# Moving two kinds of DMA issue between queues, filling products in bf16, and new orders, in a four-layer diffusion transformer kernel

## What is computed

```python
def attention(x, kv_src, w, gate):          # seven of them in all
    h = layer_norm(x) * scale + shift       # modulated in most
    q, k, v = h @ Wq + bq, kv_src @ Wk + bk, kv_src @ Wv + bv
    s = einsum("qhd,khd->hqk", q, k) / sqrt(8)
    # five attentions are over all 256 keys, one is in shifted windows of 64 tokens,
    # one keeps the 16 largest scores of each query (top_k) before the softmax
    return x + gate * (softmax(s) @ v @ Wo + bo)

def mlp(x):                                 # three of them; gelu, gelu, swiglu
    return x + gate * (act(norm(x) @ W1 + b1) @ W2 + b2)

# blocks: self + cross + mlp; self + cross + mlp; cross; window + top-16 cross + mlp
```

## Time and profile before

| | us |
|---|---|
| median of 3 runs | 686.51 (684.52 to 690.16) |
| the profiled execution | 680.88 |
| its span, first to last instruction | 679.0 |
| mean granted TensorE clock | 0.904 of full speed |

### The profile page before, as it was taken

How to read it: one execution, slowest core, us unless ns; L and a number is a source line. 1 busy time by engine, 2 the same in 40 slices (tenths; PEclk the granted TensorE clock), 3 DMA queues, 4 the chain that set the end, 5 groups by cost and what they waited for, 6 DMA issues and landing times.

```text
span 679.0 us, 14686 instructions
## 1 busy us (share of the span) xinstructions
PE 586.4 (86%) x5250; PEld 403.1 (59%) x5250; DVE 494.0 (73%) x1291; ACT 389.6 (57%) x671; POOL 242.9 (36%) x471
## 2 busy tenths in 40 slices
PE   4879999999989998999999997999668699787587
PEld 4645565566655655667656665667335478555456
DVE  3777766754668687636876547999998997799963
ACT  3557768788797868885878775345112150421133
POOL 7951422254532232345323353145111423112133
PEclk9869979999999998999999997579665799987899
DMA  9570342203241352013222234025000000000000
GB/s 322 134 188 2 96 110 65 64 2 65 64 86 42 68 123 65 1 34 95 64 64 65 65 78 113 4 57 125 7 2 0 2 9 2 2 8 1 2 1 16
DMA packets 22230, 39.25 MB, mean 58 GB/s; under 512 B 2640, under 2 KB 6800, under 8 KB 21904
## 3 DMA queue, kind: packets, MB, share of 16 engines
q1 hardware_dynamic: 20736, 37.37, 22.6%
q10 hardware_dynamic: 1424, 0.95, 0.5%
HBM read 7.96 MB, written 0.52 MB: 12 GB/s over the span
## 4 chain that ended last, share of the span: by engine, by line
PE 44%; ACT 18%; DVE 16%; DMA 8%; issue 7%; POOL 5%; ACTq 1%; SPq 1%; POOLq 0%
PE psum L1590 9%; ACT softmax_T L1290 9%; PE psum L1472 8%; PE psum L1566 6%; DMA qk_stack<-centred 6%; DVE left L1418 4%; PE psum L1536 4%; DVE top L1415 3%; DVE left L1428 3%; DVE top L1425 3%; PE psum L1636 3%; PE psum L1625 2%; PE psum L1577 2%; ACT qk_parts L1270 2%; PE psum L1505 2%
## 5 line engine op out<-in xcount | busy, mean ns | idle before, releaser
L1290 ACT ACTIVATE softmax_T<-psum 128x1024 f32<-128x1024 f32 (+1 forms) x224 | 210.8, 971 | 119.6 <-PE psum L1577 77.2
L1405 DVE TENSOR_REDUCE maxima<-psum 128x4 f32<-128x1024 f32 x160 | 189.6, 1217 | 65.1 <-PE psum L1536 64.7
L1566 PE MATMUL psum<-qk_stack 32*128 32x256 f32 (+1 forms) x896 | 113.9, 341 | 29.2 <-ACT softmax_T L1290 9.7
L1590 PE MATMUL psum<-softmax_T,values 128*32 128x256 f32 (+1 forms) x1792 | 124.7, 395 | 5.6 <-ACT softmax_T L1290 4.0
L1566 PEld LDWEIGHTS psum<-qk_stack 32*128 32x128 f32 x896 | 72.5, 201 | 76.6 <-issue 39.2
L1219 POOL TENSOR_SCALAR unpicked<-left 128x512 bf16<-128x512 f32 x64 | 39.5, 617 | 156.2 <-DVE left L1428 155.7
L1536 PE MATMUL psum<-qk_stack 32*128 32x256 f32 (+1 forms) x768 | 86.5, 331 | 8.6 <-ACT softmax_T L1290 2.8
L1179 POOL TENSOR_TENSOR qk_parts<-qk_parts 128x256 fp32r<-128x256 f32 x56 | 40.6, 727 | 113.7 <-ACT qk_parts L1273 113.5
L1590 PEld LDWEIGHTS psum<-softmax_T,values 128*32 128x32 f32 x1792 | 56.1, 116 | 39.2 <-ACT softmax_T L1290 10.4
L1472 PE MATMUL psum<-identity 128*128 128x256 f32 x248 | 68.7, 430 | 11.0 <-DVE left L1418 10.6
L1536 PEld LDWEIGHTS psum<-qk_stack 32*128 32x128 f32 x768 | 56.2, 195 | 35.9 <-issue 16.1
(11 more groups left out here) (98 smaller groups left out, 832.1 us busy)
## 6 DMA issues: line engine op xcount, KB each, us to landing
qk_stack<-qk_parts SPq DMA_DIRECT2D x112, 256.0 KB, 4.6
weights<-in_w SPq DMA_DIRECT2D x1, 1408.0 KB, 13.3
row_biases<-in_rows SPq DMA_DIRECT2D x1, 1088.0 KB, 10.4
weights<-in_w SPq DMA_DIRECT2D x2, 512.0 KB, 5.8
weights<-in_w SPq DMA_DIRECT2D x1, 832.0 KB, 8.9
qk_stack<-centred ACTq DMA_DIRECT2D x48, 8.0 KB
weights<-in_w SPq DMA_DIRECT2D x1, 768.0 KB, 6.6
weights<-in_w SPq DMA_DIRECT2D x1, 576.0 KB, 6.6
```

The lines of the kernel that those rows point to most:

```text
L1290: nc.scalar.activation(pT[:, slot, u % 2, :, 0:cols].rearrange("p (i t) n -> p i t n", t=NT), two_banks(step).rearrange("p i (t n) -> p i ...
L1405: nc.vector.tensor_reduce(rows[:, u // 4, u // 2 % 2, g:g + 2, :], ps.rearrange("p i (t k) -> p i t k", t=NT), AX_X, ALU.max).then_inc(fin, 1)
L1566: ins = nc.tensor.matmul(ps[:, i, t, 0:P if window else N], QKS[b][32 * g:32 * g + 32, s, 1, P * t:P * t + P], QKS[b][32 * g:32 * g + 32, ...
L1590: ins = nc.tensor.matmul(misc[32 * g:32 * g + 32, queries], V[:, b, t, first:first + 32], pT[:, slot, g // 2, 2 * (g % 2) + t, 0:P if wind ...
```

## The change

- **Stacks.** The 112 DMAs of the q and k stacks are tasks of POOL in place of SP: POOL issues each behind its own two subtractions.
- **Maxima.** The 64 DMAs of the maxima are tasks of SP in place of ACT. ACT keeps the copy to SBUF; SP waits for it. ACT issues no DMA in the loop any more.
- **Filling products** read the same identity as bf16 (128 rows, 256 columns). The planner's entry for one goes from 0.24 to 0.12 us, and their number from 0.95 of a gap to the smaller of 0.85 of it and 0.3 us + 0.6 of it.
- **Orders.** The planner's entries follow (a stack 1.0 us of POOL where it was 0.57 us of SP; the maxima 0.26 us of ACT and 0.57 us of SP where they were 0.95 us of ACT), and `LEAD`, `BIAS` and `EXTRA` have new values throughout, so all five orders are new.

```diff
@@ the planner's table of durations
-    ... ("sp", "load"): 0.6, ("sp", "stack"): 0.57,
+    ... ("sp", "load"): 0.6, ("pool", "stack"): 1.0,
-    ("pe", "maxima"): 0.33, ("act", "maxima"): 0.95,
+    ("pe", "maxima"): 0.33, ("act", "maxima"): 0.26, ("sp", "maxima"): 0.57,
...
-IDLE, SPARE_SHARE, SPARE_D, SPARE_CELLS = 0.3, 0.95, 0.24, 0.2133
+IDLE, SPARE_D, SPARE_CELLS = 0.3, 0.12, 0.107
...
 EXTRA = {
...
 }
@@ plan: tasks
-            stack = [task("sp", ("stack", b, l, s), t) for s in range(4)]
+            stack = [task("pool", ("stack", b, l, s), t) for s in range(4)]
...
-                        maxed[u // 4] = task("act", ("maxima", b, l, u // 4),
-                                             task("pe", ("maxima", b, l, u // 4), t), maxed.get(u // 4 - 1))
+                        t = task("act", ("maxima", b, l, u // 4), task("pe", ("maxima", b, l, u // 4), t),
+                                 maxed.get(u // 4 - 1))
+                        maxed[u // 4] = task("sp", ("maxima", b, l, u // 4), t)
...
@@ plan: how many filling products
-                spare[step] = int((s - since) * SPARE_SHARE * (1.0 if clock.rate == 1 else 1 / 1.8) / SPARE_D)
+                spare[step] = int(min(0.85 * (s - since), 0.3 + 0.6 * (s - since)) * (1.0 if clock.rate == 1 else 1 / 1.8) / SPARE_D)
...
-        if eng == "sp" and kind == "stack":
+        if eng == "pool" and kind == "stack":
             moves = max(end + TO_QUEUE, queue)
-            free[eng] = end = max(end, moves - AHEAD)
             queue = moves + STACK_TIME
...
@@ the table LEAD (samples down, layers of the chain across)
-LEAD = [[22.6, 23.7, 18.9, 23.7, 23.1, 31.1, 24.3, 23.5, 66.9, -397.7],
-        [15.8, 16.7, 15.8, 15.7, 15.6, 15.7, 16.4, 17.6, -44.9, 1073.6],
-        [7.8, 8.2, -12.2, 7.7, 7.8, 13.7, 8.3, 5.1, -29.6, -483.8],
-        [-0.3, 0.7, 0.9, -0.2, -0.4, 13.1, 0.5, 608.1, 549.0, 112.7]]
+LEAD = [[29.6, 27.3, 159.8, 27.1, 27.2, 25.2, 30.7, 27.0, 78.1, 420.1],
+        [18.3, 18.3, 18.3, 19.7, 18.7, -13.4, -10.7, -63.6, 338.4, -332.4],
+        [9.3, 9.1, 50.8, 7.5, 8.8, 525.5, 13.5, -500.4, -1.8, 224.2],
+        [1.3, 1.4, 437.2, -0.3, 0.9, -1.2, 4.4, 87.9, 52.7, -9.6]]
@@ SP's queue
-            sp.wait_ge(q_zero_s, 1)
-            sp.wait_ge(k_rows_s, 16 * SLOTS["qk"])
             for step in ORDERS["sp"]:
                 kind, b, l, u = step
-                if kind == "stack":
-                    slot = SLOT["qk", ("k_parts", b, l, 0)][0]
-                    after(sp, "pool", ("qk", b, l, 0))
-                    after(sp, "pool", ("k_parts", b, l, 0))
-                    sp.dma_start(QKS[b][:, u, :, :].bitcast(F32),
-                                 parts[32 * u:32 * u + 32, slot, :, :, :].bitcast(F32)).then_inc(stacked[b][u], 16)
+                if kind == "maxima":
+                    after(sp, "act", step)
+                    if ATTN[l]["kind"] == "topk":
+                        sp.dma_start(QKS[b][31::32, u, 0, :].bitcast(F32),
+                                     z[0:4, b, :, :].rearrange("p t f -> p (t f)")).then_inc(max_in[b], 16)
+                    else:
+                        sp.dma_start(QKS[b][31::32, 2 * u:2 * u + 2, 0, :].bitcast(F32),
+                                     z[0:NH // 2, b, :, :].rearrange("p t f -> p (t f)")).then_inc(max_in[b], 16)
@@ POOL's queue
+            pool.wait_ge(q_zero_s, 1)
+            pool.wait_ge(k_rows_s, 16 * SLOTS["qk"])
             for step in ORDERS["pool"]:
                 kind, b, l, u = step
-                if kind == "z":
+                if kind == "stack":
+                    slot = SLOT["qk", ("k_parts", b, l, 0)][0]
+                    pool.wait_ge(done["qk", "pool"], NTH["pool", ("qk", b, l, 0)])
+                    pool.wait_ge(done["k_parts", "pool"], NTH["pool", ("k_parts", b, l, 0)])
+                    pool.dma_start(QKS[b][:, u, :, :].bitcast(F32),
+                                   parts[32 * u:32 * u + 32, slot, :, :, :].bitcast(F32)).then_inc(stacked[b][u], 16)
+                elif kind == "z":
@@ ACT's queue, kind "maxima", behind the copy
-                    act.wait_ge(fin, NTH["act", step])
-                    if ATTN[l]["kind"] == "topk":
-                        act.dma_start(QKS[b][31::32, u, 0, :].bitcast(F32),
-                                      z[0:4, b, :, :].rearrange("p t f -> p (t f)")).then_inc(max_in[b], 16)
-                    else:
-                        act.dma_start(QKS[b][31::32, 2 * u:2 * u + 2, 0, :].bitcast(F32),
-                                      z[0:NH // 2, b, :, :].rearrange("p t f -> p (t f)")).then_inc(max_in[b], 16)
@@ PE's queue
                 for _ in range(SPARE.get(step, 0)):
-                    nc.tensor.matmul(psum[:, SLOT["bank", step][0], 0:2 * P], ident[:],
-                                     ident[:].rearrange("p (o c) -> p o c", o=1).broadcast_to([P, 2, P]),
-                                     start=True, stop=True)
+                    nc.tensor.matmul(psum[:, SLOT["bank", step][0], 0:2 * P], ident[:].bitcast(BF16)[:, 0:P],
+                                     ident[:].bitcast(BF16), start=True, stop=True)
```

More of the change, by code:

```diff
@@ L189 @@
 EXTRA = {
[L190 to L199, removed]
@@ L563 @@
-    ("dve", "mods"): 46.3, ("dve", "pbias"): -3.2, ("dve", "residual"): 82.1, ("dve", "scores"): -13.4,
-    ("dve", "stats"): 10.7, ("dve", "topk"): 247.8, ("dve", "topk_rest"): 79.7, ("dve", "up_gate"): -233.8,
[3 rows of a table removed]
-    ("pool", "gated"): -7.1, ("pool", "k_parts"): 47.3, ("pool", "pre"): -6.2, ("pool", "qk"): -1.5,
-    ("pool", "topk"): 62.7, ("pool", "z"): -11.4, ("sp", "load"): -261.8, ("sp", "stack"): 24.4,
-    ("sp", "store"): 6.0,
+    ("act", "context"): -21.7, ("act", "heads_out"): 106.1, ("act", "k_parts"): 0.8, ("act", "maxima"): 50.3,
@@ L571 @@
+    ("pe", "gates"): -1.7, ("pe", "mods"): -24.4, ("pe", "normed"): 0.1, ("pe", "pbias"): 4.5, ("pe", "qk"): -0.1,
+    ("pe", "residual"): 0.1, ("pe", "topk"): 38.5, ("pe", "up"): -0.3, ("pe", "up_gate"): 184.2,
+    ("pe", "values"): 0.1, ("pool", "gated"): 0.6, ("pool", "k_parts"): -3.6, ("pool", "pre"): -11.2,
+    ("pool", "qk"): 137.4, ("pool", "stack"): -3.6, ("pool", "topk"): 283.6, ("pool", "z"): -2.3,
+    ("sp", "load"): -114.6, ("sp", "maxima"): 115.5, ("sp", "store"): 42.9,
 }
@@ L714, in plan @@
                         i = u // half
[L715 to L717 removed]
+                        t2 = task("act", ("maxima", b, l, i), task("pe", ("maxima", b, l, i), t), maxed.get(0))
+                        maxed[2 * i] = maxed[2 * i + 1] = task("sp", ("maxima", b, l, i), t2)
+            prev = mixed = copied = None
             for u in range(8):
@@ L760, in plan @@
     for t in reversed(_sorted(order, deps)):
-        tail[t] = busy(t) + (transfer(t[1]) if t[1][0] == "load" else lands.get(t[1][0], 0.0) if t[0] == "sp" else 0.0) + max(
+        tail[t] = busy(t) + (transfer(t[1]) if t[1][0] == "load" else lands.get(t[1][0], 0.0) if t[0] == "sp" or t[1][0] == "stack" else 0.0) + max(
             (tail[n] + HOP for n in users[t]), default=0.0)
@@ L803, in gives @@
             yield "bank", (kind, b, l, u // 2 * 2 if kind == "mix" else u)
-        if eng == "sp" and kind == "stack" and u == 3:
+        if eng == "pool" and kind == "stack" and u == 3:
             yield "qk", ("k_parts", b, l, 0)
@@ L905, in plan @@
             land = queue + LANDS
-        elif eng == "act" and kind == "maxima":
+        elif eng == "sp" and kind == "maxima":
             land = end + TO_QUEUE + 0.3
         for r, taker in gives(t):
-            slots[r] += [((end if kind == "maxima" else land) + HOP, k, taker) for k in slot[r, taker]]
+            slots[r] += [(land + HOP, k, taker) for k in slot[r, taker]]
             slots[r].sort()
```

403 lines of the change are left out of this document (207 added, 196 removed), and 341 rows, old and new, of tables (BIAS, EXTRA).

## The result

| | before | after |
|---|---|---|
| median of 4 runs side by side | 688.34 us (684.52 to 690.41) | 668.25 us (665.29 to 671.45) |
| ratio | | 0.9739, 95% interval 0.9688 to 0.979 |
| the profiled execution | 680.88 us | 665.29 us |
| its span | 679.0 us | 663.5 us |
| mean granted TensorE clock | 0.904 | 0.863 |

The change is faster by 2.6%, 17.9 us of 686.5, where 669 us had been forecast. A ratio is taken over each kernel's fast executions alone (within 1.5% of its fastest), so it is not the quotient of the medians; of the kernel with both moves undone, further down, three of six are left out of it.

A forecast was written before the change was run, and what follows sets the result against it. POOL sets the pace to 45 us, PE to 418, DVE to 643, then a thin tail. 680.9 - 10 - 8 - 6 + 4 + 2.5 = 663.4 us profiled, 669 us as median; range 655 to 680 (52%).

The forecast's parts named there:

- Fillings, -10 us: DVE's waits for PE's top-16 products and the tail: fillings no longer overstay gaps, -10 us, bounds -4 and -17.
- Stacks on POOL, +4 and +2.5 us: POOL's queue: four issues at 1.0 us delay the start, +4; later latency and holds, with SP's hop, +2.5.
- Maxima off ACT, -8 + 1.1 us: Before 418 us: ACT freed of issuing maxima, -8 us, bounds 0 and -28.8; SP's later issue, +1.1.
- a second stretch that ends some 10 us earlier: Sign for ACT's relief: the stretch from 45 to 418 us, where PE sets the pace, ends some 10 us earlier.
- The bound of -28.8: Most that taking maxima off ACT could gain: all of PE's idle time from 45 to 418 us, 28.8 us.
- Orders, -6 us: Edge at 418 us: one sample's window layer moves under the top-16 phase, -6 us, bounds +5 and -19.
- Overlap of the phases by three samples: Rival 1, edge at 418 us: three samples' worth of order, fillings at their bound, 649 us; 14%.
- PE as the limit: Rival 2, before 418 us: PE at 92% takes over, ACT's relief worth 3 us, 684 us; 18%.
- Rival 2: PE takes over before 418 us: ACT's relief 3 us, orders nothing, fillings 6, 684 us, within 1%; 18%.
- rivals 3 and 4: POOL's queue: POOL becomes the limit, 709 us, 11%; DVE holds up POOL's issues, some 700 us, 5%.
- POOL as the limit: Rival 3, POOL's queue, first before 45 us: issues at 1.742 us, 709 us, deciding from about 1.5; 11%.
- DVE holding up POOL's issues: Rival 4, POOL's queue: each issue waits out half a DVE reduction, costing 1.6 us, some 700 us; 5%.

## Why the prediction was right, point by point

**Fillings, -10 us: right.** 6.5 us in the old orders and 10.8 in the new. The part in DVE's wait was larger than I took (11.8 of 13.8 us, I took 7) and the part in the tail smaller (the tail kept its length, 29.2 to 29.7 us, where I took 3). They end inside the gap mostly: three of them in a row took 0.50 us at 643.9 us, 0.17 each where I had 0.155 at most. At the lower clock they don't always: two took 0.61 us at 637.6 us, and the chain runs through them. "I cost the lower clock at nothing" held for the top-16 stretch: 0.71 in place of 0.78, and DVE waits less.

**Stacks on POOL, +4 and +2.5 us: the price of one issue too high, the price of holding POOL far too low.** An issue is 0.571 us, not 1.0. One reason that I gave for 1.0 was a misreading: 0.62 and 0.73 us are not POOL's smallest tensor work, its 128x2 operation takes 0.19 (the 9.48 row above). POOL's busy time rose by 63.5 us (242.9 to 306.4), not 112. In the start the first maxima came 2.0 us later, and moving the wait for the k rows gave 2.3 back: that whole delay was a wait that stands in the diff and that I had not costed, since I did not ask what was queued behind it. It is not all of the start: by 45 us PE had made 196 records in before, 177 in after and 187 with the wait moved, in orders that differ. "POOL gapless from 12 to 45 us" was wrong: 28.6 of 33 us. But in the orders of before the same move cost 42.5 us. I had charged the lateness of what stands behind POOL at its own length. It costs more: PE is a strict queue, and its clock was lower in that stretch (0.87 in place of 0.98).

**Maxima off ACT, -8 + 1.1 us: not a number of its own.** In orders that count on it the move is worth 25.7 us; in orders that don't, and with the stacks still on SP, it is a loss of 7.9. Between before and after the relief can't be seen: up to the first top-16 pass PE made 9.6 records a us in both (3613 in 375 us, 3527 in 366). The sign that I had named for it, a second stretch that ends some 10 us earlier, came true (9.1), but the 86 records fewer account for it: that is work moved behind the edge, the next term. The bound of -28.8 (all of PE's idle time) was a bound on the wrong thing: it leaves out that PE's busy time shrinks when its clock stays up, as the comparison of after (0.96) with the maxima back on ACT (0.92) shows.

**Orders, -6 us: the thing seen was right, the size not.** One sample's window layer moved under the top-16 phase, as forecast: 1402's last start behind 1416's first, four maxima moved in for 4.9 us. It took 9.1 us out of the second stretch and put 4.9 into the third, so -4 in this pair of profiles. But from before with both moves (+34.8) to after (-17.9) it is 52.7 us, of which the fillings are 6.5 to 10.8. So the orders bring 42 to 46 us given the moves. Moves and orders together are worth -7 to -11 us; my terms for them, -8, +4, +2.5 and -6, add up to -7.5. They came out right in sum only. Priced apart, as I did for the run with both moves alone (-1.5 for the moves, -6 for the orders), two errors of 36 to 40 us of opposite sign met, since orders are there to make up for what a move disturbs. That the forecast hit 668 us is to that extent luck. I could not have read either from the trace of before.

**The rivals.** Overlap of the phases by three samples: it was one. PE as the limit: its time did not come, but its mechanism is not excluded. PE is busy for 93% of the second stretch (92% before), and the stretch got shorter by holding fewer products, not by a faster PE. Rival 2 put the queues at +3.5 us together where I had -1.5, and 5 us are less than two executions of the same work differ by in that stretch; what was wrong in its sum is that it gave the fillings 6 us and the orders nothing. (Its chances have a slip too: "slower" at 15% is a point short of rivals 3 and 4, 16%.) POOL as the limit: an issue is far from 1.5 us, so it did not come; but its price was wrong. I had +40 us at 1.742 us an issue and a threshold of 1.5. At 2.1 to 2.3 it was +125, and in orders not made for it 0.57 was enough for +42. DVE holding up POOL's issues: no. They took 541 to 761 ns in all 112 cases, under a DVE that was busy for 66% of the second stretch; the 51 that lie under DVE's reductions and the 26 under an idle DVE have the same median, 571 ns. POOL's own operations took as long as before:

```profile
L1187 POOL TENSOR_TENSOR qk_parts<-qk_parts x56: 712/727/777, 18.2 to 547.6; 128x256 fp32r<-128x256 f32 x56
```

The rule of the Trainium skill ("SBUF — State Buffer", on the two separate sides) is about a VectorE instruction in a two-port mode, or one with two SBUF inputs against a GpSimd operation that reads SBUF. DVE's maxima read one operand, from PSUM, so these runs do not test it; two issues lay under line 1429, whose inputs are both in SBUF, and took 595 and 617 ns.

**What stays open.** How much the queues as such are worth. The pair (new queues, new orders) is 11.4 us (some 6 to 17) ahead of (old queues, old orders) with the same fillings; with the queues swapped in either pair it is 16 to 35 us worse; and a second set of orders for the new queues is level with the old queues in their own. The same search for the old queues, from empty tables, ends at a planned 675.7 us against 655.6, which speaks for the new queues, but plans were off by 9 to 23 us here. An equally long search on the chip's own times for both would settle it; that was not tried.

## What to carry to other kernels

Where engines are strict queues in a planned order, a moved task has no price of its own: cost it as "move plus new plan", make both single swaps before you credit either part, and read the windows of each for busy time and clock beside the waits. A wait of PE in a stretch that PE limits can cost more than its length, as the clock may be down behind it; so PE's busy time for an equal count of products belongs beside every list of waits. And whenever a loop moves to another queue, look at the waits that stand in front of the loop: they now hold work that never needed them.

## What the runs showed of the hardware that I had not expected

- GpSimd issues a plain DMA of 256 KB within SBUF in 0.54 to 0.76 us, median 0.571, no slower than SP (0.542, median 0.797, up to 1.742). To landing it is 5.1 us in the median against SP's 4.6, and 4.6 too where SP issues them in the orders of after. The difference, 0.5 us, is near the 0.4 us that the Trainium skill's page "DMA: Bandwidth & Descriptors", Specifications, gives between the two paths' first bytes. That this is the cause is not shown: with POOL held longer behind each issue its own median is 3.5 us, below SP's, so the time to landing seems to depend more on how closely the transfers follow each other than on which queue issues them.
- SP's issue of an 8 KB DMA is 0.521 us in the median in after (0.704 at most in 48), and 0.583, up to 1.704, where 256 KB transfers go through the same queue. Single long ones occur without them: up to 1.152 us with both moves in the orders of before.
- Behind a wait of 4.55 us that ended at 33 us TensorE was at 0.50 until past 65 us, where without it it was at 0.97 from 45 us on; over the whole stretch, 12 us more of idle time went with 39 us more of busy time, 4 of them for more products.
- Float32 filling products gained nothing against none: 3.0 and 5.2 us slower by the times, 1.8 and 3.7 by the profiles from the first top-16 pass on. bf16 ones gained 3.6 and 5.6 us by the times, 9.2 and 3.8 by the profiles.
